# Attention of a decoder layer in double steps: two pairs of heads at a time on one Trainium2 core

## What is computed

```python
q = (x @ Wq).reshape(N, S, HEADS, HEAD_DIM).transpose(0, 2, 1, 3)
k = (x @ Wk).reshape(N, S, HEADS, HEAD_DIM).transpose(0, 2, 1, 3)
v = (x @ Wv).reshape(N, S, HEADS, HEAD_DIM).transpose(0, 2, 1, 3)
logits = jnp.einsum('nhid,nhjd->nhij', q, k) * scale + causal
attn = jax.nn.softmax(logits, axis=-1)
out = jnp.einsum('nhij,nhjd->nhid', attn, v)
out = out.transpose(0, 2, 1, 3).reshape(N, S, HEADS * HEAD_DIM) @ Wo + bo
x = _layernorm(x + out)
```

## Time and profile before

| | us |
|---|---|
| median of 3 runs | 908.75 |
| lowest, highest run | 908.33, 1269.37 |
| profiled execution, first to last instruction | 905.5 |

### The profile page before, as it was taken

One profiled execution on the slowest core, in us unless ns is written; L12 is line 12 of the kernel. 1 busy time (PEld: TensorE's weight loads), 2 busy tenths in 40 slices (PEclk: granted clock), 3 DMA queues, 4 the chain that ended last, 5 costly groups with the idle time before them and its releaser, 6 DMA issues. The chain is left out here.

```text
span 905.5 us, 23841 instructions
## 1 busy us (share of the span) xinstructions
PE 876.6 (97%) x8190; PEld 669.9 (74%) x8190; DVE 648.3 (72%) x1839; ACT 557.3 (62%) x1347; POOL 365.5 (40%) x492
## 2 busy tenths in 40 slices
PE   5999999999999999999999999999999999999996
PEld 4777777777777777776767676676788888888864
DVE  5667787867676777667878786869677766776655
ACT  6778776767666677656575755545455555554555
POOL 2333433333333465325444442354534444444433
PEclk9999999999999999999999999999999999999998
DMA  9742434242423241230000000099443332333226
GB/s 320 195 141 96 163 107 151 94 142 93 140 76 125 95 150 49 9 94 2 1 1 2 1 1 1 32 356 409 135 107 49 49 49 44 49 49 48 43 30 192
DMA packets 61584, 88.09 MB, mean 97 GB/s; under 512 B 17279, under 2 KB 46527, under 8 KB 61343
## 3 DMA queue, kind: packets, MB, share of 16 engines
q1 hardware_dynamic: 53439, 75.52, 25.3%
q0 software_dynamic: 7488, 10.27, 7.3%
q10 hardware_dynamic: 544, 0.79, 0.3%
HBM read 56.00 MB, written 30.56 MB: 96 GB/s over the span
## 5 line engine op out<-in xcount | busy, mean ns | idle before, releaser
L2257 PE MATMUL ps<-slots,e 128*128 128x128 f16 x1872 | 189.9, 219 | 2.2 <-DVE xs L2424 2.2
L669 POOL TENSOR_SCALAR prob<-prob,rden 128x128 f32<-128x128 f32 (+1 forms) x256 | 110.7, 448 | 200.9 <-DVE rden L958 200.9
L2257 PEld LDWEIGHTS ps<-slots,e 128*128 x1872 | 152.4, 97 | 35.4 <-issue 5.1
L855 ACT ACTIVATE prob<-prob,nmx 128x128 f32<-128x128 f32 (+1 forms) x256 | 114.1, 450 | 40.8 <-DVE nmx L951 37.9
L2265 PE MATMUL ps<-e,xT 128*128 x312 | 117.3, 378 | 0.0
L2354 ACT ACTIVATE slots<-slots 128x512 f32<-128x512 f32 x78 | 49.2, 631 | 107.0 <-DVE slots L2408 107.0
L31 PE MATMUL ps<-xT,wqkv 128*128 128x256 f16 x768 | 96.1, 275 | 0.4 <-DVE wqkv L938 0.4
L31 PEld LDWEIGHTS ps<-xT,wqkv 128*128 128x128 f16 x768 | 70.4, 98 | 29.6 <-issue 21.7
L2266 PE MATMUL ps<-e,xT 128*128 x312 | 85.1, 273 | 0.0
L1769 POOL DMA_INDIRECT xg<-rows_x,dst x39 | 40.9, 1049 | 106.5 <-DVE mask L2397 103.2
L951 DVE CUSTOM_DVE_ANT_0 prob<-ps,mask 128x128 f32<-128x128 f32 (+1 forms) x256 | 75.9, 353 | 3.9 <-PE ps L749 3.9
(11 more groups left out here) (275 smaller groups left out, 1939.0 us busy)
## 6 DMA issues: line engine op xcount, KB each, us to landing
halves<-parted SPq DMA_DIRECT2D x36, 512.0 KB, 2.9
piece<-in_L_ffn_ew SPq DMA_DIRECT2D x32, 512.0 KB, 4.5
e<-halves SPq DMA_DIRECT2D x16, 1024.0 KB, 15.4
piece<-in_L_ffn_sh_w SPq DMA_DIRECT2D x4, 512.0 KB, 9.4
sw<-halves SPq DMA_DIRECT2D x4, 512.0 KB, 6.3
rows_x<-xs SPq DMA_DIRECT2D x4, 512.0 KB, 7.7
xs<-back_y SPq DMA_DIRECT2D x8, 256.0 KB, 5.0
out<-xs SPq DMA_DIRECT2D x8, 256.0 KB, 2.1
```

The costliest lines, as they stand in the source:

```text
L669: PO.tensor_scalar(prob[m % 3][:, h, r], prob[m % 3][:, h, r], rden[m % 2][:, h, t:t + 1], 1.0, ALU.mult, ALU.mult).then_inc(normed, 1)
L855: SC.activation(p, p, ACT.Exp, bias=nmx[u][:, h, t:t + 1], scale=-1.0, accum_out=den[u][:, h, t:t + 1]).then_inc(exped, 1)
L2257: yield PE.matmul(ps[:, 2 * u + q, (k % 4) * P:(k % 4) * P + P], w[ch][h], xgT[u][j][:, ch, :], start=n == 0, stop=n == 3 * DC - 1)
```

## The change

A step now handles a double: two pairs of heads of one batch. `STAGES` = 32 doubles take the place of 64 items.

- `scores(m)` makes both pairs' scores, into banks 2 and 3 and banks 4 and 5. Right behind it stands `weigh_values(m - 2)` for both pairs, into bank 1, which it shares with `project_v`. Behind these the projections of queries and keys for one pair, the output projection, the projections for the other pair, `turn_prob` for both pairs (12 transposes, into banks 2 to 5) and `project_v`.
- `queries` and `keys` become one copy of 512 columns (`queries_keys`), the scale moves to the mask. The copies of the turned probabilities become 2 x 384 columns on DVE and 2 x 384 on ACT; `heads_high` and `heads_low` become 512 columns each.
- `masks`, `exponentials`, `reciprocals` and `normalise` do the same per head as before, in the order of both pairs.
- The tables for pieces, preparing shares and weights are rewritten for steps of double length. The `qk` tiles move into the later slots' buffer; `prob` has two buffers of four heads.

```diff
-            HIGH_AT = {-2: (3,), -1: (4,), 0: (5,), 2: (6,), 3: (7,), 5: (8,), 7: (9,)}
-            LOW_AT = {-1: (3,), 0: (4,), 1: (5,), 2: (6,), 3: (7,), 5: (8,), 7: (9,)}
+            HIGH_AT = {-2: (3,), -1: (4, 5), 0: (6,), 1: (7,), 2: (8,), 3: (9,)}
+            LOW_AT = {-1: (3, 4), 0: (5, 6), 1: (7,), 2: (8,), 3: (9,)}
...
             def room(j):
 
-                return (j % PAIRS != 3, 0, 2 - (j % PAIRS == 4) - 2 * (j % PAIRS == 3))
-            LOW_FROM = 4
+                return (2, 2 - (j % DOUBLES == 1), 2 - 2 * (j % DOUBLES == 1) - (j % DOUBLES == 0))
+            LOW_FROM = 2
```

PE's functions and its loop:

```diff
                 def turn_prob(m):
-                    PE.wait_ge(normed, 4 * (m + 1))
-                    if m >= 1:
-                        PE.wait_ge(o_hi, m)
-                        PE.wait_ge(o_lo, m)
-                    for h in range(2):
-                        for blk in range(3):
-                            mm = PE.transpose(ps[:, 4 + h, blk * P:blk * P + P],
-                                              prob[m % 3][:, h, blk * P:blk * P + P], ident[:, :])
-                    mm.then_inc(p_turned, 1)
+                    if m + 1 < STAGES:
+                        PE.wait_ge(masked, 8 * (m + 2))
+                    for p in range(2):
+                        PE.wait_ge(normed, 8 * m + 4 * (p + 1))
+                        for h in (2 * p, 2 * p + 1):
+                            for blk in range(3):
+                                mm = PE.transpose(ps[:, 2 + h, blk * P:blk * P + P],
+                                                  prob[m % 2][:, h, blk * P:blk * P + P], ident[:, :])
+                        mm.then_inc(p_turned, 1)
...
                 def scores(m):
 
-                    PE.wait_ge(qk_out, 2 * (m + 1))
-                    if m >= 1:
-                        PE.wait_ge(masked, 4 * m)
-                    for t in range(2):
-                        for h in range(2):
-                            r = slice(HD * h, HD * h + HD)
-                            mm = PE.matmul(ps[:, 2 + h, query_tile(t)], qk[m % 2][r, 0, t * P:t * P + P],
-                                           qk[m % 2][r, 1, 0:(t + 1) * P], start=True, stop=True)
-                    mm.then_inc(s_mm, 1)
+                    if m >= 2:
+                        PE.wait_ge(pT_out, 2 * (m - 1))
+                    for p in range(2):
+                        PE.wait_ge(qk_out, 2 * m + p + 1)
+                        for t in range(2):
+                            for h in range(2):
+                                r = slice(HD * h, HD * h + HD)
+                                mm = PE.matmul(ps[:, 2 + 2 * p + h, query_tile(t)], qk[p][r, 0, t * P:t * P + P],
+                                               qk[p][r, 1, 0:(t + 1) * P], start=True, stop=True)
+                        mm.then_inc(s_mm, 1)
...
                 def weigh_values(m):
                     PE.wait_ge(pT_out, 2 * (m + 1))
-                    PE.wait_ge(v_out, m // 2 + 1)
-                    for t, key, at in ((0, 0, 0), (1, 0, P), (1, 1, 2 * P)):
-                        for h in range(2):
-                            r = slice(HD * h, HD * h + HD)
-                            mm = PE.matmul(ps[r, 4 + t, 384:512], v_sb[m // 2 % 2][:, key, m % 2, r],
-                                           pT[:, h, at:at + P], start=key == 0, stop=key == t, skip_group_check=True)
+                    PE.wait_ge(v_out, min(m + 2, STAGES))
+                    for p in range(2):
+                        for t, key, at in ((0, 0, 0), (1, 0, P), (1, 1, 2 * P)):
+                            for h in range(2):
+                                r = slice(HD * h, HD * h + HD)
+                                mm = PE.matmul(ps[r, 1, (2 * p + t) * P:(2 * p + t) * P + P], v_sb[m % 2][:, key, p, r],
+                                               pT[:, 2 * p + h, at:at + P], start=key == 0, stop=key == t,
+                                               skip_group_check=True)
                     mm.then_inc(o_mm, 1)
...
-                    if 0 <= j - 1 < ITEMS:
-                        turn_prob(j - 1)
-                    if 0 <= j + 1 < ITEMS:
+                    if 0 <= j + 1 < STAGES:
                         scores(j + 1)
-                    if j == ITEMS:
-                        vw_tensor(1)
-                    if j + 2 < ITEMS:
-                        project_qk(j + 2)
-                    if 0 <= j - 1 < ITEMS:
+                    if 0 <= j - 1 < STAGES:
+                        if j == LAST:
+                            vw_tensor(0)
+                            vw_tensor(1)
                         weigh_values(j - 1)
-                    if j + 1 < ITEMS and j % 2 == 1:
-                        project_v(j + 1)
-                    if j == ITEMS - 1:
-                        vw_tensor(0)
-                    if output_share(j) is not None:
-                        output_projection(*output_share(j))
+                    if j + 2 < STAGES:
+                        project_qk(2 * (j + 2))
                     if share_at(j) is not None:
-                        turned = min(X_EARLY + (j + 4) // PAIRS, NB)
+                        turned = min(X_EARLY + (j + 2) // DOUBLES, NB)
                         PE.wait_ge(x_hi, turned)
                         PE.wait_ge(x_lo, turned)
                         prep_tensor(share_at(j))
+                    if j == LAST:
+                        vw_tensor(2)
+                        vw_tensor(3)
+                    if 0 <= j - 1 < STAGES:
+                        output_projection(j - 1)
+                    if j + 2 < STAGES:
+                        project_qk(2 * (j + 2) + 1)
+                    if 0 <= j < STAGES:
+                        turn_prob(j)
+                    if 0 <= j + 1 < STAGES:
+                        project_v(j + 1)
                     if batch_turned(j) is not None:
                         PE.wait_ge(x_hi, batch_turned(j))
                         PE.wait_ge(x_lo, batch_turned(j))
                         turn_inputs(batch_turned(j))
-                vw_tensor(2)
-                vw_tensor(3)
```

```diff
+                def queries_keys(n):
                     SC.wait_ge(qk_mm, n + 1)
                     if n >= 2:
                         SC.wait_ge(s_mm, n - 1)
-                    SC.mul(qk[n % 2][:, 0, :], ps[:, 0, 0:S], SCALE / WS).then_inc(qk_out, 1)
-
-                def keys(n):
-                    SC.mul(qk[n % 2][:, 1, :], ps[:, 0, S:2 * S], 1 / WS).then_inc(qk_out, 1)
+                    SC.mul(qk[n % 2][:, :, :], ps[:, 0, :].rearrange("p (k t) -> p k t", k=2), 1 / WS).then_inc(qk_out, 1)
 
                 def probs_turned(m):
 
-                    SC.wait_ge(p_turned, m + 1)
+                    SC.wait_ge(p_turned, 2 * m + 2)
                     if m >= 1:
                         SC.wait_ge(o_mm, m)
-                    SC.copy(pT[:, 1, :], ps[:, 5, 0:384]).then_inc(pT_out, 1)
+                    SC.copy(pT[:, 2:4, :], ps[:, 4:6, 0:384]).then_inc(pT_out, 1)
 
...
                 for j in range(FIRST, LAST + 1):
-                    if 0 <= j - 1 < ITEMS:
-                        probs_turned(j - 1)
+                    if 0 <= j + 1 < STAGES:
+                        exponentials(j + 1, 0)
+                    if j == LAST:
+                        vw_high(0)
+                        vw_high(1)
+                    if 0 <= j - 1 < STAGES:
+                        heads_high(j - 1)
+                    if 0 <= j + 1 < STAGES:
+                        exponentials(j + 1, 1)
+                    if j + 2 < STAGES:
+                        queries_keys(2 * (j + 2))
                     for q in high_at.get(j, ()):
...
+                        prep_scalar(share_at(j), 6)
                     for i in HIGH_AT.get(j, ()):
                         weight_high(i)
-                    if 8 <= j < 8 + NB:
-                        context_squares(j - 8)
-                    share = share_at(j - 1)
-                    if share is not None and share >= KEYS and j < ITEMS - 1:
...
                         high_part(0)
+                    if 0 <= j < STAGES:
+                        probs_turned(j)
                     if batch_turned(j) is not None:
                         inputs_high(batch_turned(j))
-                    if j == ITEMS:
-                        vw_high(0)
-                        vw_high(1)
-                        squared_slots(0)
```

DVE has the same order of parts; its loop begins, and `probs_turned` and `values_out` stand, so:

```diff
                 def probs_turned(m):
 
-                    VE.wait_ge(p_turned, m + 1)
+                    VE.wait_ge(p_turned, 2 * m + 1)
                     if m >= 1:
                         VE.wait_ge(o_mm, m)
-                    VE.tensor_copy(pT[:, 0, :], ps[:, 4, 0:384]).then_inc(pT_out, 1)
+                    VE.tensor_copy(pT[:, 0:2, :], ps[:, 2:4, 0:384]).then_inc(pT_out, 1)
...
                 weight_low(2)
                 VE.wait_ge(const_cut, 3)
                 for j in range(FIRST, LAST + 1):
-                    if 0 <= j - 1 < ITEMS:
```

(20 more changed lines are left out.)

220 lines of the change are left out of this document (108 added, 112 removed).

## The result

| | before | after |
|---|---|---|
| median, us | 908.76 | 922.19 |
| profiled execution, us | 905.5 | 920.9 |
| last matmuls of the attention stage end, us | 376.1 | 389.6 |

Slower: 13.4 us by the two medians, which is 1.5%; the ratio on record, taken over the undisturbed runs and so without one run of the kernel before of 1269.37 us, is 1.0159, with a 95% interval of 1.0146 to 1.0172. That is within the 2% that counted as no change, in the forecast's range and in its direction; but +13.4 us is twice the +6.4 that I had put.

The account below looks back on a forecast made before the run. Attention was taken as bound by TensorE's stream, its saved 21 us turning into waits on ACT and DVE: first scores +1.4, first two double steps +1.1, other 29 +0.6, tail +3.3, together +6.4, 908.75 to 915 us; range 899 to 928.

Parts of the forecast that it names:

- TensorE's work of two pairs, 9.65: TensorE's attention work per double step: 9.65 us with joined blocks instead of 10.30, 21 us less over 32 steps.
- the price of one more change of kind: On TensorE between scores and weighing: one change of kind still counted, 0.1 us a step.
- The serial chain makes it 10.35: ACT's and DVE's evacuations make TensorE wait ahead of output projection and second projection: plain step 10.35 us, against 10.30 before.
- The steps with a long share: Eight double steps with a long preparation share (keys, products of weights) take 11.30 us each.
- The wait for pieces, 8.0: ACT waits for a second expert piece's load at j = 3, 7, 11, ...: seven places, five at 1.6, 8 us.
- The batch's turn, 7.6 net: Turning six batches' inputs: transposes and a wait 0.5, ACT and DVE 0.9, 6 x 1.4 = 8.4 us, some 0.8 hidden.
- The first scores, +1.4: Start of attention: two projections and two evacuations stand ahead of the first scores instead of one, +1.4 us.
- The first two double steps, +1.1: First two double steps take 8.6 and 9.9, 18.5 us against 17.4 before: +1.1 us.
- The tail, +3.3: End of attention: 22.4 us of work and some 3 of waits against 22.1 before, +3.3 us.
- Nothing after the stage: Everything behind attention's last matmuls is unchanged: 0 us.
- The prediction's own sign of being wrong: Wrong if plain steps near 9.7, waits for pieces missing, or start and tail together cost much more than 6 us.

Follow-up runs that it names:

- e1_turn_first: The changed kernel with the turning of the probabilities, and ACT's copy of them, set ahead of the output projection: 905.57 us, ratio to before 0.9979.
- e7_best: The changed kernel with e1_turn_first, e3_fill, e4_inputs_first, a step's second piece behind the second evacuation, and DVE's probabilities copy ahead of casts and later shares: 893.22 us.
- e4_inputs_first: The changed kernel with the four transposes of the next batch's inputs set ahead of the projection of values: 915.92 us, ratio to before 1.0096.
- e9_add_first: The changed kernel with DVE's addition of a finished batch set ahead of its copy of the turned probabilities: 921.52 us, ratio to before 1.0158.
- e5_busy_pe: The changed kernel with 22 identity transposes ahead of the projections for the fourth and sixth pair, keeping TensorE busy: 921.20 us, ratio to before 1.0147.
- e3_fill: The changed kernel with ACT's queries and keys evacuation between the two pairs' exponentials in steps -1 and 0 alone: 918.89 us, ratio to before 1.0120.
- e6_split_qk: The changed kernel with ACT's evacuation of queries and keys in two copies of 256 columns again: 923.09 us, ratio to before 1.0172.
- e2_pieces_late: The changed kernel with ACT's high halves of the expert pieces moved to the end of a step: 915.99 us, ratio to before 1.0095.

## Why the prediction was off, point by point

- *TensorE's work of two pairs, 9.65.* Right: 9.63 where nothing waits (e1_turn_first, e7_best), and the price of one more change of kind, put at 0.1, measured 0.1 to 0.16.
- *The serial chain makes it 10.35.* Right in size and place: 10.32, waits of 0.47 and 0.20 (start to start), removed by work put in front of them. The steps with a long share were 11.24 (keys) and 11.36 (products of weights) against 11.30. By these the 29 steps would be 307.1; I had 307.8.
- *The wait for pieces, 8.0.* Right in mechanism and place: seven places at j = 3, 7, 11 and so on, 11.5 us of ACT; 7.8 us of the 29 steps went with them. That this is so near 8.0 is in part luck, since 1.3 of it is the clock (below). Which places paid was off: at j = 11 it was DVE and not the piece, and at j = 19 a long step didn't hide it.
- *The batch's turn, 7.6 net.* What I had in it came true: the transposes cost 0.44 in each of six steps (2.6) and the evacuations behind them 4.9 (e4_inputs_first), 7.5 together. What failed is the list: DVE's addition of the finished batch stands in the same place of the same queue, ahead of values and masks, and the sum has no term for it and gives no reason. It cost 3.2 (e9_add_first). That is all of the 29 steps' surplus over the forecast; smaller ones (0.8 at j = 11, 0.7 less by the plain steps) cancel.
- *The first scores, +1.4.* Right in some executions, not in this one. The second projection and the scores of the kernel after, and then those of e1_turn_first, whose instructions up to here are the same:

```profile
13.82 2.74 PE L31 MATMUL ps<-xT,wqkv 128*128 128x256 f16 x12 [0.69 <-ACT slots L870]
16.49 2.03 PE L750 MATMUL ps<-slots 64*128 64x128 f32 x16
```

```profile
13.96 1.49 PE L31 MATMUL ps<-xT,wqkv 128*128 128x256 f16 x12 [0.69 <-ACT slots L870]
15.38 1.68 PE L750 MATMUL ps<-slots 64*128 64x128 f32 x16
```

  At half rate the projection takes 2.67 to the next start, at full rate 1.42. The memory traffic doesn't make the difference: from 14 to 15 us the DMA share was 1.09 to 1.11 in both. In three of the ten profiles with double steps it was at full rate and the first scores began at 15.4, +1.5 on before; in the others at 16.5 to 17.0. I had charged it at the price of mid-attention and given no range for the clock's start.
- *The first two double steps, +1.1.* This step of the prediction failed by 2.0. The first was 9.10 against 8.6, by scores that were still at the slow rate (1.97 for 1.51). The second was 11.35 against 9.9; kept busy it took 9.84 (e5_busy_pe). Its whole surplus of 1.5 is TensorE's return at the lower clock, which I had priced at nothing, without a reason.
- *The wait at 69 to 71 us* for a piece, 2.14, did the same: scores and weighing behind it took 2.34 and 2.25 from start to start instead of 1.51 and 1.46. This is 1.6, of which 0.3 came back in the same step; it is in the pieces' 7.8, so the waits for pieces themselves were 6.5.
- *The tail, +3.3.* +3.9, near enough.
- *Nothing after the stage.* +1.9: the barrier's wait on PE's own queue is 1.5 instead of 0.7, and near 577 us one wait for GpSimd is 2.10 where it was 1.04 in the same code. The barrier's part is open (it is 1.5 in all ten kernels with double steps). The other shows in DVE's rows: a cast of four columns, first before, then after, with the GpSimd instruction beside the latter.

```profile
555.36 0.17 DVE L1567 CAST crec<-crec 128x4 f16<-128x4 f32 x1
```

```profile
569.68 1.24 DVE L1570 CAST crec<-crec 128x4 f16<-128x4 f32 x1
569.63 1.26 POOL L1500 TENSOR_TENSOR dl<-slots,nn 128x512 f32<-128x512 f32 x1 [5.31 <-ACT nn L1380]
```

  The cast begins 0.05 behind GpSimd's instruction and ends with it; before, it was over when that one began. All ten kernels with double steps have this 1.24 and the wait of 2.10, so it belongs to the change and not to one execution. It reaches PE by way of DVE, ACT and GpSimd. That GpSimd's instruction holds the cast is read from these times and not tested.

So the mechanism of the chain and of the pieces was right, and what failed are terms of the sum: the first scores and the first two double steps, where TensorE at half rate was priced at nothing, and the batch's turn, which lacked the addition. The prediction's own sign of being wrong, a start and a tail that cost much more than 6, came true: together 9.6. By the profiled executions the sum was 9 short (15.4 against 6.4): 3.2 up to the end of the first two steps, all of it TensorE at half rate (1.7 at the program's start, where only the spacings show it, and 1.5 behind an idle time, where the granted clock does), 3.2 for the addition, 0.6 in the tail and 1.9 behind the stage. By the medians it was 7 short.

## What to carry to other kernels

When a change makes the busiest engine's work shorter, write the longest chain through the other engines beside it, and then look for independent work to put in front of each wait: here one group moved, with ACT's copy behind it, was worth 16.6 us, more than the change had cost. Merging steps also merges their small duties in one queue, and everything that stands ahead of an evacuation there (a bunched load, an addition once per batch, all the exponentials in the first steps) has to be listed. Price the beginning of a program by rows of the beginning.

## What the hardware showed that I hadn't expected

- TensorE's granted clock fell to 0.50, which is 1.2 GHz, for about 3 us after some idle times in the middle of a busy stream, and the work behind took 1.3 to 1.6 us more. It isn't certain at any length seen: of the 18 waits of 2.0 to 2.9 us in this stage of the ten kernels with double steps, 11 were followed by a fall and 7 weren't. The shortest with a fall was 2.05 (e3_fill), the longest without one 2.93 (the changed kernel). In the same place near 70 us the clock fell in the changed kernel, e3_fill, e5_busy_pe and e6_split_qk behind 2.05 to 2.14 us, and stayed at 1.00 in e4_inputs_first and e9_add_first behind 2.15 and 2.02. After waits of up to 1.9 us it never fell.
- At the program's start TensorE works at half its later rate (0.213 from one matmul of a projection to the next, then 0.109), although the granted clock reads 1.00 there. When it rises differs in the same code: second projections that started at 13.96 to 14.02 were fast in three executions, ones at 13.82 to 14.29 slow in the seven others, and there the first scores were slow too, wholly or in part (1.96 to 2.86 for 1.51). The Trainium skill (TensorE: Matmul & The Clock Gate, Part 1) says that the point of the rise differs from run to run; these rows agree. The price here was 1.7 to 2.0 us: from the second projection's start to the second double's scores it took 10.06 and 10.11 where it was fast (e1_turn_first, e6_split_qk) and 11.77 to 12.05 where it was slow (the changed kernel, e2_pieces_late, e9_add_first).
- A DVE cast of four columns took 1.24 us instead of 0.17 when it began 0.05 us behind a GpSimd instruction of 1.26, and one us of it reached TensorE. Shifting a stage in time can set up such a meeting in code that nobody changed.
